# Graph-network kernel: four gather buffers instead of three, two PSUM banks for the sums, loops of four chunks

## The chip, the cores and the metric

One Trainium2 chip, one core of it. The metric is the device time of one execution in microseconds (us), the median of several. One profiled execution supplies the trace.

## What is computed

`N` = 6250 nodes with 256 features each, `E` = 100000 edges that are sorted by destination, four heads of 64. Two graph-attention layers run one after the other, beside them one linear attention over the nodes, and behind them a mixture of 16 experts (two per node). Cut to what matters here:

```
def gat_conv(x, src, dst, W, a_src, a_dst, b):
    h = (x @ W).reshape(-1, H, C)
    e = leaky_relu(alpha_s[src] + alpha_d[dst], 0.2)
    m = segment_max(e, dst)
    ex = exp(e - m[dst])
    s = segment_sum(ex, dst)
    out = segment_sum(h[src] * (ex / s[dst])[:, :, None], dst)
    return out + b

x = x + gat(relu(gat(xn))) + mix(xn)
x = x + experts(layernorm(x))
```

The `mix` part needs, over all nodes, the product of normalised keys and values (`dots`). Its keys and values are computed tile by tile inside the edge stage of the first layer.

## The kernel before

The program is a row of stages: prepare, project the inputs, find the maxima per destination, the edge stage of layer 0 (`gat_edges`, about 180 to 1400 us of the span), the maxima again, the edge stage of layer 1 (about 1435 to 2640 us), then the order of the experts, the experts and the finish (to the end).

An edge stage runs over `NC` = 98 chunks of 1024 edges and `NT` = 49 tiles of 128 nodes, one tile for every second chunk. Each engine writes its own instruction stream out by hand: `skewed` gives every engine a list of steps with an offset each, and turn t of an engine runs each step for chunk t minus its offset (for the tile steps only where that number is even, for the tile of half that number). The first and last turns are written out, the middle is a hardware loop with a body of 2 x `SLOTS` = 6 chunks, so that every buffer number is a constant in it.

What a chunk needs, in order:

- SP: `load` fetches the chunk's 1024 source numbers (`idx`, L880), after `logits` of the chunk three before. `load_codes` (L884) fetches the destination codes of the next chunk, spread to 128 partitions, after `hotT` of the chunk before. In layer 0 `load_x` (L894, offset 1) fetches the transposed node features of tile i after the keys and the values of tile i-3 have been computed, because there are `SLOTS` = 3 buffers `xnT`. In layer 1 `load_x` stands at offset 6 and waits for a much older step.
- POOL: `gather` issues 8 indirect DMAs of 128 rows by 260 fp32 (L926) into one of three buffers `G` ("gathered" in the trace). It waits for the chunk's `idx` and for `added` of the chunk three before, that is for the matmuls that read the buffer last.
- DVE: `edge_logits` (L974 reads the PSUM bank of `targets`, L977 adds the gathered part, L978, L979), `placed` (L983, the fp32 one-hot `hotf`, three buffers, waits for `added` of three before), `edge_scale` (L990, multiplies the gathered rows by the weights from ACT), `one_hot` of the chunk two ahead (L966 `hotT`, L607 and L608 `dwin`), `gain` of the chunk two before (L998, twice: PSUM sums into `acc`), and tile work (L1007, L1023, L1029 to L1032).
- PE: `targets` (L1204), keys (L1226), project, turn, dots (L1234), then `add` of the chunk before (L1212, the sum of 8 matmuls into one of three banks `psA`; it waits for `hotf`, for `scaled` and for `gain` of the chunk three before), values (L1220).

The wait for `gain` and the count that stands ready for it at the start are these:

```
dve.sem_inc(s["acc"], 2 * SLOTS)
pe.wait_ge(s["acc"], g * 2 + 2)
```

In layer 0 `targets` shares its bank with the weights, so PE waits there for `scaled` of the chunk before it.

Of the kernel before, what the change touches and what calls it, by code (L numbers as in the profile page):

```python
# [23 lines left out]
ds = bass.ds  # L24
# [10 lines left out]
CE = KT * P  # L35
SLOTS = 3
NC = -(-E // CE)
# [98 lines left out]
def build(nc, a, out):  # L136
# [15 lines left out]
    with ExitStack() as top:  # L152
# [27 lines left out]
        with ExitStack() as gnn:  # L180
# [6 lines left out]
            sq, ks = w1[:, 2], w1[:, 3, 0]  # L187
            vs = [w1[:, 11 + b, 0] for b in range(SLOTS)]
            xnT = [w1[:, 4 + b, 0, 0:C] for b in range(SLOTS)]
            wq, woutT, zmix = (w1[:, e].rearrange("p a (b f) -> p (a b) f", f=C) for e in (8, 9, 10))  # L190
# [565 lines left out]
def gat_edges(nc, layer, srcp, table, codes_d, partition, iota, acc, own, peak, parts, windows, attention, last, sem):  # L756
# [5 lines left out]
    with ExitStack() as ctx:  # L762
# [21 lines left out]
        rden = sb("rden", [P, H])  # L784
        psA = pb("psA_e", [P, SLOTS, 512])
        if attention:
            xnT_d, eps, wkvT, wq, woutT, zmix, sq, ks, vs, xnT, dotsT, mixM = attention
            a, table_out, ident, dtab, wext, scratch = last
            ss = sb("ss", [P, 3, 2 * MH])
            rkv = sb("rkv", [P, MH])  # L790
            psDW = pb("psDW_e", [P, 512])
            psD, psW = psDW[:, 0:6 * KT * H].rearrange("p (k c h) -> p k c h", c=3, h=H), psDW[:, 256:256 + KT * H]
            psKV = pb("psKV", [P, 2, MI])
            psM = pb("psM", [P, 512])
            psF = pb("psF", [P, 512])
            hidden, hidT = scratch[:, 0:C], scratch[:, C:2 * C].rearrange("p (k f) -> p k f", k=2)
            bias = scratch[:, 2 * C:2 * C + 2]
        else:
            a, xnT_d, xf_d, moe_d, ident, ones, eps, mixM, pair_hot, extra, w1, weights_in, scratch = last
            psD = pb("psD_e", [P, 2 * KT, 3, H])  # L800
            psW = pb("psW_e", [P, KT * H])
            psY = pb("psY", [P, 512])
            psX = pb("psX2", [P, 512])
            psG = pb("psG", [P, 512])
            taken = [0]

            def part(n):
                taken[0] += n
                return scratch[:, taken[0] - n:taken[0]]
            x = [part(C) for b in range(SLOTS)]  # L810
            xnT = [part(C) for b in range(SLOTS)]
# [12 lines left out]
        names = ["idx_in0", "idx_in1", "idx_in2", "g_in0", "g_in1", "g_in2", "codes_in0", "codes_in1", "hotT", "hotf", "targets", "dwin", "own", "own_weights",  # L824
                 "own_terms", "target_read", "logits", "weights", "scaled", "added", "acc", "pass", "dests", "dest_steps", "vsteps", "logit_steps", "tick",
                 "nears", "constants", "rden", "hidden", "fin_turned", "end"]
        if attention:
            names += ["xn_in0", "xn_in1", "xn_in2", "keys_ps", "values_ps", "squared", "kvsum", "kvroot", "ks", "vs", "dots", "key",
                      "relu", "projected", "out", "stored"]
        else:  # L830
            names += ["x_in0", "x_in1", "x_in2", "mixed", "halves", "moments", "yb", "root", "inverse", "scale", "xf", "stored", "xfT", "gated",
                      "gate_logits", "number", "gap", "exp", "bias"]
        s = {n: sem(f"g{layer}_{n}") for n in names}
        block = ctx.enter_context(nc.Block())
        assert NC == 2 * NT
        PER_STORE = 16 if attention else 32

        def chunks(eng, begin, end, *stages):
# [3 lines left out]
            with eng.Fori(0, rounds) as r:  # L842
                def told(step):
                    return lambda c, k, u: step(r * NC + c, c, k % SLOTS, k % 2, r * len(range(k % SLOTS, NC, SLOTS)) + u * 2 + k // SLOTS)

                def tile_of(step):

                    def even(c, k, u):
                        if k % 2 == 0:
                            b = k // 2  # L850
                            step(r * NT + (u * SLOTS + b), u * SLOTS + b, b, r * len(range(b, NT, SLOTS)) + u)
# [90 lines left out]
        def _(dve):  # L942
            dve.sem_inc(s["logits"], SLOTS)
            dve.sem_inc(s["target_read"], 1)
            dve.sem_inc(s["acc"], 2 * SLOTS)
            dve.sem_inc(s["hotT"], 2)
# [16 lines left out]
            def one_hot(g, c, q, par, use):  # L963
# [4 lines left out]
                chain.at(g * STEPS)  # L968
                blend(dve, chain, dwin[:, q, :], half[:, q, :], parts, tile, lower[:, ds(c, 1)], upper[:, ds(c, 1)]).then_inc(s["dwin"], 1)

# [21 lines left out]
            def gain(g, c, q, par, use):  # L992
                first = dve.value_load(window_tile[0:1, ds(c, 1)], min_val=0, max_val=NT)
                dve.wait_ge(s["added"], g + 1 + SLOTS)
                for half_of, mask in enumerate((lower, upper)):
                    dve.wait_ge(s["acc"], g * 2 + 2 * SLOTS)
                    into = acc[:, ds(first + half_of, 1), :].rearrange("p o f -> p (o f)")
                    dve.scalar_tensor_tensor(into, psA[:, q, 0:GW], mask[:, ds(c, 1)], into, ALU.mult, ALU.add).then_inc(s["acc"], 1)  # L998

            def denominators(t, i, b, use):  # L1000

                dve.wait_ge(s["hidden"], t + 1)
                if attention:
                    dve.wait_ge(s["out"], t * 2 + 2)
                hold(dve, s["acc"], t * 4 + (4 if isinstance(i, int) and i == NT - 1 else 6) + 2 * SLOTS, s["tick"])
                d = dest_of(dve, i)
                dve.reciprocal(rden[:], acc[:, ds(d, 1), C:GW].rearrange("p o h -> p (o h)")).then_inc(s["rden"], 1)  # L1007

            def next_pass(r):

                dve.wait_ge(s["acc"], r * (2 * NC) + 2 * NC + 2 * SLOTS)
                dve.tensor_scalar(code_r[:], code_r[:], -SPREAD, None, ALU.add).then_inc(s["pass"], 1)
# [7 lines left out]
            if attention:  # L1020
# [4 lines left out]
                def keys(t, i, b, use):  # L1025
# [4 lines left out]
                    key.link(dve.tensor_tensor(rkv[:], ss[:, 2, 0:MH], ss[:, 2, MH:2 * MH], ALU.mult))  # L1030
                    dve.wait_ge(s["dots"], t + SLOTS)
                    dve.tensor_tensor(ks.rearrange("p (g d) -> p g d", d=MD), psKV[:, 0, :].rearrange("p (g d) -> p g d", d=MD),  # L1032
# [5 lines left out]

                hold(dve, s["dots"], rounds * NT + SLOTS, s["tick"])
                for hp in range(4):  # L1040
# [7 lines left out]
            else:  # L1048
                steps = Chain(dve, s["end"])

                def stats(t, i, b, use):
                    hold(dve, s["mixed"], t + 1 + SLOTS, s["tick"])
                    dve.bn_stats(st, psY[:, 0:C]).then_inc(s["halves"], 1)
# [46 lines left out]
        def _(act):  # L1100
# [9 lines left out]
            def divide(t, i, b, use):  # L1110
                d = dest_of(act, i)
                act.wait_ge(s["rden"], t + 1)
                if not attention:
                    act.wait_ge(s["yb"], t + 1)
                act.wait_ge(s["fin_turned" if attention else "mixed"], t + (1 if attention else SLOTS))
                for h in range(H):
# [3 lines left out]
            if attention:  # L1120
                def squares(t, i, b, use):
                    act.wait_ge(s["keys_ps"], t + 1 + SLOTS)
                    act.wait_ge(s["values_ps"], t + 1 + SLOTS)
                    act.wait_ge(s["kvsum"], t + 1)
# [31 lines left out]
            else:  # L1156
                act.wait_ge(s["codes_in1"], 16)
                act.wait_ge(s["idx_in2"], 16)
                for e in range(0, NX - 4, 4):
# [33 lines left out]
        def _(pe):  # L1193
# [3 lines left out]
            def targets(g, c, q, par, use):  # L1197
# [5 lines left out]
                for k in range(KT):  # L1203
                    ins = pe.matmul(psD[:, 2 * k:2 * k + 2, :, :].rearrange("p g c h -> p (g c h)"), hotT[:, par, k, :], dwin[:, q, :], start=True, stop=True)  # L1204
                ins.then_inc(s["targets"], 1)

            def add(g, c, q, par, use):
# [3 lines left out]
                for k in range(KT):  # L1211
                    ins = pe.matmul(psA[:, q, 0:GW], hotf[:, q, k, :], G[:, q, k, :], start=(k == 0), stop=(k == KT - 1))  # L1212
                ins.then_inc(s["added"], 1)

            if attention:
# [29 lines left out]
                def project(t, i, b, use):  # L1245
# [19 lines left out]
            else:  # L1265
# [17 lines left out]
                def gates(t, i, b, use):  # L1283
# [4 lines left out]
                    ins.then_inc(s["gated"], 1)  # L1288
                pe.sem_inc(s["mixed"], SLOTS)
                pe.sem_inc(s["gated"], 1)  # L1290
# [469 lines left out]
```

## Time and profile before

| | |
|---|---|
| median of 3 runs | 3246.72 us (3243.73 to 3248.16) |
| profiled execution, its own time | 3252.82 us |
| its span in the profile | 3251.2 us |
| mean granted TensorE clock | 0.817 |
| PE busy | 2138.4 us, 66% |
| PE weight load busy | 1632.7 us, 50% |
| DVE busy | 1829.3 us, 56% |
| ACT busy | 931.8 us, 29% |
| POOL busy | 1934.7 us, 60% |

The shares are averages over stages that have different limits. Idle time before an instruction is put down to a releaser: another engine's instruction, a DMA, "remote" (a semaphore whose sender the profile doesn't name) or "issue" (nothing that the profile shows).

### The profile page before, as it was taken

The page shows a single profiled execution, that of the slowest core. Times are in us where ns is not written, and L with a number is a line of the kernel's source. Part 1 is how long each engine was busy: PE and PEld are TensorE (multiplying, and loading weights), DVE is VectorE, ACT ScalarE, POOL GpSimd, SP SyncE. Part 2 cuts the span into 40 slices and gives each one's busy share as a digit, 9 for nine tenths or more (in the row PEclk, how much of TensorE's full clock was granted, in tenths as well). Part 3 has the DMA queues.
Part 4 walks back from the last instruction along what each step waited for, and adds up shares of the span by engine and source line. Part 5 has one row for each costly group of instructions (what it writes and reads, how often), then busy time and mean ns, then how long its engine had stood idle before and what let it go on. Part 6 is the DMA issues. An engine that isn't in the chain of part 4 may idle for free. (4 is left out here: it accounts for less than half of the span.)

```text
span 3251.2 us, 50978 instructions
## 1 busy us (share of the span) xinstructions
PE 2138.4 (66%) x10263; PEld 1632.7 (50%) x10264; DVE 1829.3 (56%) x4382; ACT 931.8 (29%) x2254; POOL 1934.7 (60%) x1918
## 2 busy tenths in 40 slices
PE   1736676666666666635656666666576556999996
PEld 1424454444444444424444444444454436999984
DVE  5555565556556565555555555555555556555545
ACT  0502233223222232210122222222222224444445
POOL 0356666666666666626666666666666622676654
PEclk9968878778788888867777777777777778999998
DMA  3734444444444444425544444544445425555555
GB/s 82 212 94 118 119 120 119 123 123 118 118 121 116 118 120 121 114 78 170 134 132 133 134 128 128 139 128 136 131 128 139 131 72 141 104 104 105 103 93 168
DMA packets 273929, 399.38 MB, mean 123 GB/s; under 512 B 90592, under 2 KB 187255, under 8 KB 273849
## 3 DMA queue, kind: packets, MB, share of 16 engines
q0 software_dynamic: 101728, 251.76, 31.3%
q1 hardware_dynamic: 128457, 101.17, 11.4%
q10 hardware_dynamic: 43680, 45.76, 4.3%
q8 instruction: 21, 0.34, 0.0%
q14 instruction: 43, 0.35, 0.0%
HBM read 344.28 MB, written 54.62 MB: 123 GB/s over the span
## 5 line engine op out<-in xcount | busy, mean ns | idle before, releaser
L926 POOL DMA_INDIRECT gathered<-table,idx x1568 | 1583.7, 1010 | 808.9 <-issue 467.5
L1212 PE MATMUL psA_e<-gathered,hotf 128*128 128x260 f32 x3136 | 871.8, 437 | 93.8 <-issue 59.2
L1212 PEld LDWEIGHTS psA_e<-gathered,hotf 128*128 128x128 f32 x3136 | 692.3, 224 | 244.4 <-issue 115.6
L1107 ACT ACTIVATE gathered<-t_e 128x32 f32<-128x32 f32 x196 | 45.0, 230 | 1062.3 <-issue 649.4
L1623 POOL DMA_INDIRECT moe_d<-xscaled,xtarget x113 | 179.2, 1586 | 123.7 <-DVE xtarget L1567 54.8
L983 DVE TENSOR_TENSOR hotf<-iota,code_r 128x1024 f32<-128x1024 bf16 x196 | 240.2, 1226 | 5.1 <-issue 5.1
L998 DVE SCALAR_TENSOR_TENSOR acc<-psA_e,lower,acc 128x260 f32 x196 | 95.8, 489 | 259.4 <-issue 203.3
L1204 PE MATMUL psDW_e<-dwin,hotT 128*128 128x24 bf16 x784 | 38.4, 177 | 290.9 <-DVE gathered L990 236.1
L1595 PEld LDWEIGHTS xpsH<-xxT,w1e 128*128 128x128 f32 x1808 | 221.5, 193 | 6.2 <-ACT xxT L1524 0.4
L990 DVE TENSOR_TENSOR gathered<-gathered,psW_e 128x2048 f32<-128x2048 f32 x98 | 223.5, 2280 | 1.7 <-ACT gathered L1107 1.7
L990 DVE TENSOR_TENSOR gathered<-gathered,psDW_e 128x2048 f32<-128x2048 f32 x98 | 223.4, 2280 | 0.0
L1604 PE MATMUL xpsO<-w,hidT 128*128 x904 | 217.2, 383 | 7.8 <-DVE hidT L1556 7.2
L1595 PE MATMUL xpsH<-xxT,w1e 128*128 128x128 f32 x1808 | 222.1, 276 | 0.0
L1204 PEld LDWEIGHTS psDW_e<-dwin,hotT 128*128 128x128 bf16 x784 | 33.8, 101 | 345.7 <-issue 314.8
L1204 PE MATMUL psD_e<-dwin,hotT 128*128 128x24 bf16 x784 | 42.7, 175 | 220.6 <-issue 149.7
L1226 PE MATMUL psKV<-w 128*128 128x512 f32 x196 | 158.8, 956 | 41.6 <-DVE w L1032 40.1
L1556 DVE TENSOR_SCALAR hidT<-xpsH,b1T 128x128 f32<-128x128 f32 x452 | 127.4, 345 | 93.0 <-issue 43.0
L1604 PEld LDWEIGHTS xpsO<-w,hidT 128*128 128x128 f32 x904 | 163.8, 191 | 29.3 <-issue 11.0
L1220 PE MATMUL psKV<-w 128*128 128x512 f32 x196 | 115.4, 718 | 67.9 <-ACT w L1127 41.2
L977 DVE TENSOR_TENSOR z_e<-both_e,gathered 128x32 f32<-128x32 f32 x196 | 38.2, 195 | 209.0 <-DMA gathered<-table,idx 161.3
L1204 PEld LDWEIGHTS psD_e<-dwin,hotT 128*128 128x128 bf16 x784 | 35.2, 98 | 229.5 <-issue 193.3
L1614 POOL DMA_INDIRECT xx<-xf_d,xsource x113 | 111.4, 986 | 40.9 <-issue 33.0
(314 smaller groups left out, 3213.7 us busy)
## 6 DMA issues: line engine op xcount, KB each, us to landing
codes<-codes_d SPq DMA_DIRECT2D x196, 256.0 KB
gathered<-table,idx POOLq DMA_INDIRECT x1568
w<-in_L_ffn_w ACTq DMA_DIRECT2D x8, 2048.0 KB
xb<-in_L_ffn_b SPq DMA_DIRECT2D x113, 128.0 KB
w<-xnT_d SPq DMA_DIRECT2D x98, 128.0 KB
table<-acc POOLq DMA_DIRECT2D x49, 130.0 KB
table<-acc ACTq DMA_DIRECT2D x49, 130.0 KB
xnT_d<-xnT ACTq DMA_DIRECT2D x49, 128.0 KB
```

The costliest lines, as they stand in the source:

```text
L926: pool.indirect_dma_start(out=G[:, q, k, :], out_offset=None, in_=table, in_offset=bass.IndirectOffsetOnAxis(ap=idx[:, q, k:k + 1], axis=0 ...
L983: dve.tensor_tensor(hotf[:, q, :, :], iota[:].rearrange("p (k f) -> p k f", k=1).to_broadcast([P, KT, P]), code_r[:, ds(c * KT, KT)].rearr ...
L990: dve.tensor_tensor(f, f, w, ALU.mult).then_inc(s["scaled"], 1)
L1204: ins = pe.matmul(psD[:, 2 * k:2 * k + 2, :, :].rearrange("p g c h -> p (g c h)"), hotT[:, par, k, :], dwin[:, q, :], start=True, stop=True)
L1212: ins = pe.matmul(psA[:, q, 0:GW], hotf[:, q, k, :], G[:, q, k, :], start=(k == 0), stop=(k == KT - 1))
L1220: ins = pe.matmul(psKV[:, 1, :], xnT[b][:, kc * P:(kc + 1) * P], wkvT[:, kc, 1, :], start=(kc == 0), stop=(kc == 1))
L1226: ins = pe.matmul(psKV[:, 0, :], xnT[b][:, kc * P:(kc + 1) * P], wkvT[:, kc, 0, :], start=(kc == 0), stop=(kc == 1))
L1556: dve.tensor_scalar(hidT[:, q % 2, k * P:(k + 1) * P], psH[:, q % 2, k * P:(k + 1) * P], b1T[:, ds(e, 1), k:k + 1].rearrange("p o k -> p ( ...
L1595: ins = pe.matmul(psH[:, q % 2, k * P:(k + 1) * P], w1e[:, q % 2, kc, k * P:(k + 1) * P], xT[:, q % 2, kc, :], start=(kc == 0), stop=(kc = ...
L1604: ins = pe.matmul(psO[:, q % 2, 0:C], hidT[:, q % 2, k * P:(k + 1) * P], w2[:, ds(e, 1), k, :].rearrange("p o f -> p (o f)"), start=(k == ...
L1614: pool.indirect_dma_start(out=x[:, q, :], out_offset=None, in_=xf_d, in_offset=bass.IndirectOffsetOnAxis(ap=source[:, q:q + 1], axis=0)).t ...
L1623: pool.indirect_dma_start(out=moe_d, out_offset=bass.IndirectOffsetOnAxis(ap=target[:, q % 2:q % 2 + 1], axis=0), in_=scaled[:, q % 2, :], ...
```

## The change

Three things change together.

- `SLOTS` goes from 3 to 4. It now numbers the buffers of `G`, `hotf` and `idx` alone. `gather` waits for `added` of the chunk four before, `load` for `logits` of four before.
- What belongs to a tile (`xnT`, `x`, `vs`) goes from three buffers to `TURN` = 2, `dwin` and `half` from three to two, and `psA` from three banks to two. `load_x` of tile i waits for keys and values of tile i-2, and `add` waits for `gain` of the chunk two before.
- The loop body goes from 6 chunks to 4 (`SLOTS`). The offsets of the steps stay as they are.

```
-SLOTS = 3
+SLOTS = 4
+TURN = 2
...
-            vs = [w1[:, 11 + b, 0] for b in range(SLOTS)]
-            xnT = [w1[:, 4 + b, 0, 0:C] for b in range(SLOTS)]
+            vs = [w1[:, 11 + b, 0] for b in range(TURN)]
+            xnT = [w1[:, 4 + b, 0, 0:C] for b in range(TURN)]
...
-        dwin = sb("dwin", [P, SLOTS, 6 * H], BF16)
-        half = sb("half", [P, SLOTS, 6 * H], BF16)
+        dwin = sb("dwin", [P, 2, 6 * H], BF16)
+        half = sb("half", [P, 2, 6 * H], BF16)
...
-        psA = pb("psA_e", [P, SLOTS, 512])
+        psA = pb("psA_e", [P, 2, 512])
...
-                skewed(eng, NC, 2 * SLOTS, 2, 2, [(o, tile_of(step) if by_tile else told(step)) for o, step, *by_tile in stages])
+                skewed(eng, NC, SLOTS, 2, 2, [(o, tile_of(step) if by_tile else told(step)) for o, step, *by_tile in stages])
...
-            dve.sem_inc(s["acc"], 2 * SLOTS)
+            dve.sem_inc(s["acc"], 4)
...
-                    dve.wait_ge(s["acc"], g * 2 + 2 * SLOTS)
+                    dve.wait_ge(s["acc"], g * 2 + 4)
                     into = acc[:, ds(first + half_of, 1), :].rearrange("p o f -> p (o f)")
-                    dve.scalar_tensor_tensor(into, psA[:, q, 0:GW], mask[:, ds(c, 1)], into, ALU.mult, ALU.add).then_inc(s["acc"], 1)
+                    dve.scalar_tensor_tensor(into, psA[:, par, 0:GW], mask[:, ds(c, 1)], into, ALU.mult, ALU.add).then_inc(s["acc"], 1)
...
-                ins = pe.matmul(psA[:, q, 0:GW], hotf[:, q, k, :], G[:, q, k, :], start=(k == 0), stop=(k == KT - 1))
+                ins = pe.matmul(psA[:, par, 0:GW], hotf[:, q, k, :], G[:, q, k, :], start=(k == 0), stop=(k == KT - 1))
...
-                pe.sem_inc(s["dots"], SLOTS)
-                pe.sem_inc(s["values_ps"], SLOTS)
-                pe.sem_inc(s["keys_ps"], SLOTS)
+                pe.sem_inc(s["dots"], TURN)
+                pe.sem_inc(s["values_ps"], TURN)
+                pe.sem_inc(s["keys_ps"], TURN)
```

Two places in the order of instructions matter below. The first is SP's queue in the loop of layer 0. Semaphore names in brackets are those under which a number was first used; `g0_keys_ps,g0_values_ps` are the keys and values of this stage, the others stand for `logits` (before the fetch of `idx`) and for `hotT` (before the fetch of the codes). Before, at the end of the loop of six:

```order
96 L892 ISA
97 L894 ISA [waits g0_keys_ps,g0_values_ps]
98 L894 DMA w<-xnT_d 128x256
99 L880 REGISTER_ALU [waits i_first]
100 L880 DMA idx<-srcp 128x8
101 L59 ISA
102 L884 ISA [waits e_tiled]
103 L884 DMA codes<-codes_d 128x1024
104 L107 REGISTER_ALU
105 L107 COMPARE_AND_BRANCH
```

With the change, at the end of the loop of four:

```order
83 L893 ISA
84 L895 ISA [waits g0_keys_ps,g0_values_ps]
85 L895 DMA w<-xnT_d 128x256
86 L881 REGISTER_ALU [waits i_tick]
87 L881 DMA idx<-srcp 128x8
88 L60 ISA
89 L885 ISA [waits e_coded]
90 L885 DMA codes<-codes_d 128x1024
91 L108 REGISTER_ALU
92 L108 COMPARE_AND_BRANCH
```

The order has stayed: the fetch of the features of a tile, and behind it the fetch of the next even chunk's source numbers and of the codes. What moved is the tile whose keys and values the first one waits for, from i-3 to i-2.

The second is POOL's queue in the same stage. Before, three of the six gathers in the loop body (each with its wait for `idx` in the row ahead):

```order
71 L59 ISA [waits e_filled]
72 L926 DMA gathered<-table,idx 128x260 [waits g0_added]
73 L926 DMA gathered<-table,idx 128x260 x7
74 L59 ISA [waits e_loaded]
75 L926 DMA gathered<-table,idx 128x260 [waits g0_added]
```

With the change, the start of a body that holds four of them:

```order
65 L108 UNCONDITIONAL_BRANCH
66 L108 ISA
67 L60 ISA [waits e_stored]
68 L927 DMA gathered<-table,idx 128x260 [waits g0_added]
69 L927 DMA gathered<-table,idx 128x260 x7
```

Each chunk has the same 8 DMAs and the same two waits as before; the body has 12 rows where it had 18, and `g0_added` is waited for at a count that is lower by one chunk.

## Rows read from the trace of the kernel before

**Rows 1.** Windows: us, each engine's busy time (instructions), clock, DMA share, GB/s.

```profile
180.00:1400.00 1220.00, 799.55 (x3408) 544.27 (x3409) 707.10 (x1324) 339.23 (x817) 796.50 (x784) 0.81 0.43 117
...
1435.00:2640.00 1205.00, 729.52 (x3110) 557.43 (x3110) 662.80 (x1371) 257.56 (x667) 787.23 (x784) 0.75 0.49 135
```

**Rows 2.** Costliest groups on the page: busy, mean ns of one, idle before.

```profile
L926 POOL DMA_INDIRECT gathered<-table,idx x1568 | 1583.7, 1010 | 808.9 <-issue 467.5
```

**Rows 3.** Waits of POOL, 180 to 1400 us: total, times, longest.

```profile
POOL gathered L926 <- remote: 152.8, 48, 4.7
```

**Rows 4.** The same waits, 1435 to 2640 us.

```profile
POOL gathered L926 <- remote: 152.6, 44, 4.3
```

**Rows 5.** Timeline of POOL, 600 to 760 us (start, us, operation, count, idle before).

```profile
612.49 0.95 POOL L926 DMA_INDIRECT gathered<-table,idx  x1 [3.43 <-remote]
...
729.32 0.95 POOL L926 DMA_INDIRECT gathered<-table,idx  x1 [0.31 <-issue]
733.31 0.95 POOL L926 DMA_INDIRECT gathered<-table,idx  x1 [3.05 <-remote]
...
743.03 0.95 POOL L926 DMA_INDIRECT gathered<-table,idx  x1 [0.30 <-issue]
...
757.65 0.94 POOL L926 DMA_INDIRECT gathered<-table,idx  x1 [2.96 <-remote]
```

**Rows 6.** Timeline of PE, 712 to 742 us.

```profile
714.82 3.67 PE L1212 MATMUL psA_e<-gathered,hotf 128*128 128x260 f32 x16
725.51 0.37 PE L1204 MATMUL psDW_e<-dwin,hotT 128*128 128x24 bf16 x8 [7.02 <-DVE gathered L990]
...
731.96 3.67 PE L1212 MATMUL psA_e<-gathered,hotf 128*128 128x260 f32 x16
...
739.28 3.01 PE L1212 MATMUL psA_e<-gathered,hotf 128*128 128x260 f32 x13
```

**Rows 7.** Timeline of DVE, 717 to 747 us.

```profile
732.45 0.49 DVE L998 SCALAR_TENSOR_TENSOR acc<-psA_e,lower,acc 128x260 f32 x1 [4.83 <-issue]
732.86 0.48 DVE L998 SCALAR_TENSOR_TENSOR acc<-psA_e,upper,acc 128x260 f32 x1
733.25 0.35 DVE L974 TENSOR_REDUCE both_e<-psDW_e 128x64 f32<-128x192 f32 x1
...
739.95 0.48 DVE L998 SCALAR_TENSOR_TENSOR acc<-psA_e,upper,acc 128x260 f32 x1
...
745.80 0.19 DVE L977 TENSOR_TENSOR z_e<-both_e,gathered 128x32 f32<-128x32 f32 x1 [2.85 <-DMA gathered<-table,idx]
```

**Rows 8.** Timeline of SP's queue, 712 to 760 us.

```profile
715.81 0.70 SPq L894 DMA_DIRECT2D w<-xnT_d  x1
722.25 0.71 SPq L880 DMA_DIRECT2D idx<-srcp  x1
...
740.12 0.00 SPq L894 DMA_DIRECT2D w<-xnT_d  x1
```

**Rows 9.** Timeline of POOL, 826 to 880 us.

```profile
829.93 0.94 POOL L926 DMA_INDIRECT gathered<-table,idx  x1 [3.04 <-remote]
...
861.41 0.94 POOL L926 DMA_INDIRECT gathered<-table,idx  x1 [0.30 <-issue]
867.06 0.96 POOL L926 DMA_INDIRECT gathered<-table,idx  x1 [4.71 <-remote]
```

**Rows 10.** Timeline of DVE, 826 to 895 us.

```profile
865.93 0.36 DVE L974 TENSOR_REDUCE both_e<-psDW_e 128x64 f32<-128x192 f32 x1 [14.65 <-remote]
...
875.37 0.35 DVE L974 TENSOR_REDUCE both_e<-psDW_e 128x64 f32<-128x192 f32 x1
```

**Rows 11.** Timeline of SP's queue, start of the stage.

```profile
179.57 0.45 SPq L880 DMA_DIRECT2D idx<-srcp  x1
```

**Rows 12.** Timeline of POOL, the first gather.

```profile
183.54 2.77 POOL L926 DMA_INDIRECT gathered<-table,idx  x1 [5.68 <-issue]
```

**Rows 13.** Waits of SP's queue, 180 to 1400 us.

```profile
SPq L60 <- DVE t_e L979: 241.5, 48, 14.8
```

More of the change, by code:

```diff
@@ L809, in part @@
                 return scratch[:, taken[0] - n:taken[0]]
-            x = [part(C) for b in range(SLOTS)]
-            xnT = [part(C) for b in range(SLOTS)]
+            x = [part(C) for b in range(TURN)]
+            xnT = [part(C) for b in range(TURN)]
             hidden, xf, xfT, beta, gate = part(C), part(C), part(C), part(C), part(2 * NX).rearrange("p (k e) -> p k e", k=2)
@@ L823, in gat_edges @@
             one = sb("one", [P, NT])
-        names = ["idx_in0", "idx_in1", "idx_in2", "g_in0", "g_in1", "g_in2", "codes_in0", "codes_in1", "hotT", "hotf", "targets", "dwin", "own", "own_weights",
+        names = ["idx_in0", "idx_in1", "idx_in2", "idx_in3", "g_in0", "g_in1", "g_in2", "g_in3", "codes_in0", "codes_in1", "hotT", "hotf", "targets", "dwin", "own", "own_weights",
                  "own_terms", "target_read", "logits", "weights", "scaled", "added", "acc", "pass", "dests", "dest_steps", "vsteps", "logit_steps", "tick",
@@ L834, in gat_edges @@
         block = ctx.enter_context(nc.Block())
-        assert NC == 2 * NT
+        assert NC == 2 * NT and SLOTS == 2 * TURN
         PER_STORE = 16 if attention else 32
@@ L843, in told @@
                 def told(step):
-                    return lambda c, k, u: step(r * NC + c, c, k % SLOTS, k % 2, r * len(range(k % SLOTS, NC, SLOTS)) + u * 2 + k // SLOTS)
+                    return lambda c, k, u: step(r * NC + c, c, k, k % 2, r * len(range(k, NC, SLOTS)) + u)
                 def tile_of(step):
@@ L850, in even @@
                             b = k // 2
-                            step(r * NT + (u * SLOTS + b), u * SLOTS + b, b, r * len(range(b, NT, SLOTS)) + u)
+                            step(r * NT + (u * TURN + b), u * TURN + b, b, r * len(range(b, NT, TURN)) + u)
                     return even
                 begin(r)
-                skewed(eng, NC, 2 * SLOTS, 2, 2, [(o, tile_of(step) if by_tile else told(step)) for o, step, *by_tile in stages])
+                skewed(eng, NC, SLOTS, 2, 2, [(o, tile_of(step) if by_tile else told(step)) for o, step, *by_tile in stages])
                 end(r)
@@ L968, in one_hot @@
                 chain.at(g * STEPS)
-                blend(dve, chain, dwin[:, q, :], half[:, q, :], parts, tile, lower[:, ds(c, 1)], upper[:, ds(c, 1)]).then_inc(s["dwin"], 1)
+                blend(dve, chain, dwin[:, par, :], half[:, par, :], parts, tile, lower[:, ds(c, 1)], upper[:, ds(c, 1)]).then_inc(s["dwin"], 1)
             def edge_logits(g, c, q, par, use):
@@ L1004, in denominators @@
                     dve.wait_ge(s["out"], t * 2 + 2)
-                hold(dve, s["acc"], t * 4 + (4 if isinstance(i, int) and i == NT - 1 else 6) + 2 * SLOTS, s["tick"])
+                hold(dve, s["acc"], t * 4 + (8 if isinstance(i, int) and i == NT - 1 else 10), s["tick"])
                 d = dest_of(dve, i)
@@ L1009, in next_pass @@
             def next_pass(r):
-                dve.wait_ge(s["acc"], r * (2 * NC) + 2 * NC + 2 * SLOTS)
+                dve.wait_ge(s["acc"], r * (2 * NC) + 2 * NC + 4)
                 dve.tensor_scalar(code_r[:], code_r[:], -SPREAD, None, ALU.add).then_inc(s["pass"], 1)
@@ L1030, in keys @@
                     key.link(dve.tensor_tensor(rkv[:], ss[:, 2, 0:MH], ss[:, 2, MH:2 * MH], ALU.mult))
-                    dve.wait_ge(s["dots"], t + SLOTS)
+                    dve.wait_ge(s["dots"], t + TURN)
                     dve.tensor_tensor(ks.rearrange("p (g d) -> p g d", d=MD), psKV[:, 0, :].rearrange("p (g d) -> p g d", d=MD),
@@ L1037, in _ @@
                 rounds = chunks(dve, both_new(dve), next_pass, (1, edge_logits), (1, placed), (1, edge_scale), (6, keys, True), (-1, one_hot), (3, gain), (5, denominators, True), (5, sums, True))
-                hold(dve, s["dots"], rounds * NT + SLOTS, s["tick"])
+                hold(dve, s["dots"], rounds * NT + TURN, s["tick"])
                 for hp in range(4):
@@ L1051, in stats @@
                 def stats(t, i, b, use):
-                    hold(dve, s["mixed"], t + 1 + SLOTS, s["tick"])
+                    hold(dve, s["mixed"], t + 1 + TURN, s["tick"])
                     dve.bn_stats(st, psY[:, 0:C]).then_inc(s["halves"], 1)
@@ L1114, in divide @@
                     act.wait_ge(s["yb"], t + 1)
-                act.wait_ge(s["fin_turned" if attention else "mixed"], t + (1 if attention else SLOTS))
+                act.wait_ge(s["fin_turned" if attention else "mixed"], t + (1 if attention else TURN))
                 for h in range(H):
@@ L1121, in squares @@
                 def squares(t, i, b, use):
-                    act.wait_ge(s["keys_ps"], t + 1 + SLOTS)
-                    act.wait_ge(s["values_ps"], t + 1 + SLOTS)
+                    act.wait_ge(s["keys_ps"], t + 1 + TURN)
+                    act.wait_ge(s["values_ps"], t + 1 + TURN)
                     act.wait_ge(s["kvsum"], t + 1)
@@ L1157, in _ @@
                 act.wait_ge(s["codes_in1"], 16)
-                act.wait_ge(s["idx_in2"], 16)
+                act.wait_ge(s["idx_in3"], 16)
                 for e in range(0, NX - 4, 4):
@@ L1203, in targets @@
                 for k in range(KT):
-                    ins = pe.matmul(psD[:, 2 * k:2 * k + 2, :, :].rearrange("p g c h -> p (g c h)"), hotT[:, par, k, :], dwin[:, q, :], start=True, stop=True)
+                    ins = pe.matmul(psD[:, 2 * k:2 * k + 2, :, :].rearrange("p g c h -> p (g c h)"), hotT[:, par, k, :], dwin[:, par, :], start=True, stop=True)
                 ins.then_inc(s["targets"], 1)
@@ L1288, in gates @@
                     ins.then_inc(s["gated"], 1)
-                pe.sem_inc(s["mixed"], SLOTS)
+                pe.sem_inc(s["mixed"], TURN)
                 pe.sem_inc(s["gated"], 1)
```

4 lines of the change are left out of this document (2 added, 2 removed).

## The prediction

> **What bounds the kernel now.** I read the windows by stage first, then the waits of POOL in the two edge stages, then the timelines of POOL, PE, DVE and SP over two chunks. The edge stages take 1220 and 1205 us of the 3251.2 us span [rows 1]; the change touches nothing else. No engine is full in them. POOL is busy 796.5 and 787.2 us for 784 instructions [rows 1], 1010 ns each [rows 2], and the gap behind each gather is 0.30 us [rows 5]: a chunk of 8 gathers takes about 10.4 us and 98 of them 1020 us, more than PE's 800 or DVE's 707. POOL is the engine to look at, and what it loses beyond its own rate are the waits called "remote": 152.8 us in 48 places in layer 0, 152.6 us in 44 in layer 1 [rows 3, 4]. That is 3.2 to 3.5 us once in two chunks. The timeline shows the rhythm: seven resumes from 612.49 to 757.65 us, six periods, 24.2 us each [rows 5], that is 16 gathers (20.8 us) and one stop.
>
> **What ends a stop.** By the code the gather that resumes at 733.31 waits for the sum of the chunk three before. PE issued that sum at 714.82 and it took 3.67 us [rows 6], so it was done at 718.5, 15 us before the gather started. DVE's read at 733.25 [rows 7] waits for the small matmuls of 725.51 + 0.37 [rows 6], done 7 us before. Two waiters on two engines that were served long before, and both start just after POOL has stopped: its last gather ended at 729.32 + 0.95 = 730.27 [rows 5], DVE's `gain` starts at 732.45, the read at 733.25 [rows 7], the gather at 733.31. I read this so: while gathers run one behind the other, notices of completion from other engines arrive late, and they come in together some 2.2 us after the last gather. SP's queue has the same mark: a DMA issue takes 0.70 and 0.71 us at 715.81 and 722.25, none at 740.12 [rows 8]. By this reading a stop isn't a want of buffers, or only on its face: what POOL waits for was done, and it is the stop itself that lets the notice through.
>
> **The change, part by part**, against the profiled 3252.8 us (the median lies 6 us lower).
>
> *Four gather and one-hot buffers, layer 1.* If the reading holds, a fourth buffer lets POOL run on with a chunk more in hand once, but DVE and PE get their notices no sooner: they still work off about two chunks per stop, so POOL soon stands as often as before. Gain 0. Its bound on the other side is that all stops go: 152.6 us here, 152.8 us in layer 0, 305 us together.
>
> *Where the rule of the skill points.* The profile shows the same 3.2 to 3.5 us gap every two chunks on the engine nearest to saturation [rows 3, 4]. The Trainium skill, "Perfetto Trace Analysis", section Optimization Strategy, says that consistent bubbles on the engine that should be saturated can mean that SBUF or PSUM is short for the next tile; by that rule the change is right and the 305 us are within reach. It speaks against my forecast and is the first rival. The rows speak against it, because the buffer's last reader was done 15 us before the stop ended.
>
> *Two tile buffers, layer 0.* This is where I see a cost. SP's queue holds, in turn 2i+1, `load_x` of tile i, and right behind it the source numbers of chunk 2i+2. `load_x` now waits for the keys of tile i-2, which PE issues at its own turn 2i+1; before it waited for those of tile i-3, two turns earlier. So SP can't fetch the source numbers of an even chunk until PE has come to keys one turn before that chunk, and by the reading above SP hears of it only at the next stop. POOL's fourth buffer is of no use to the even chunks. Before, SP's main wait was for the logits of DVE (241.5 us in 48 places [rows 13]), ahead of the fetch itself and not ahead of `load_x`, which left the next numbers ready when the stop ended. Now a stop for an even chunk is, in a row: 2.2 us until the notice is there [rows 5, 7], 0.7 us for the issue of `load_x`, 0.7 us for that of `idx` [rows 8], about 2 us until the numbers are in SBUF, 0.3 us to start [rows 5]. The landing of `idx` is not in the trace by itself. Its lower bound is a gather's, from 743.03 + 0.95 = 743.98 [rows 5] to DVE's use at 745.80 [rows 7], 1.8 us; its upper bound is the first of the stage, from 179.57 + 0.45 = 180.02 to 183.54 [rows 11, 12], 3.5 us. I take 2.0, near the lower one, for the queue is short in the loop and cold at the start. The sum is 5.9 us against 152.8 / 48 = 3.2 before: +2.7 us a pair, times 47 pairs in the loop, 127 us. Stretches in which POOL stops for other reasons or runs three chunks on end [rows 9] won't pay it; I take three quarters, **+95 us**. Bounds: 0, if the numbers are there in time, and 47 x (2.7 + 1.5) = 197 us with the slow landing everywhere.
>
> *Two PSUM banks.* `add` of a chunk now waits for `gain` of two before, which DVE makes in the same turn in which it scales the chunk. PE issues the sum at 731.96, and the gain of that turn ends at 732.86 + 0.48 = 733.34: 1.4 us later. In the next turn 739.28 against 739.95 + 0.48 = 740.43: 1.15 us [rows 6, 7]. Behind `add` on PE stand the values and the next `targets`. DVE read the targets of 725.88 only at 733.25 and waits for a gather's landing at 745.80, so the shift is covered; if that cover were gone it would cost 1.3 us x 196 chunks = 250 us. DVE waits with `gain` for the sum, the sum for the gain of two before: no ring, but less play, where a notice is late. I put **+10 us** for both layers, near the covered end, with 0 and 250 us as ends.
>
> *`dwin`, `half` by parity:* both are written a turn ahead and read by the turn's `targets`, and DVE writes them again only behind its own read of that `targets` in the same turn, so no wait is added. 0. *Loops of four:* the same operations for each chunk, 12 rows of POOL in a body for 18; the branch comes every 4 chunks instead of 6, 7 more times in each stage on every engine, at the 0.30 us of a gap [rows 5] some 4 us for both, and beside other work. 0.
>
> The sum: +95 + 10 = +105 us, 3358 us for the profiled execution and **3352 us** for the median.
>
> **Rivals.**
>
> *A: the stops are a want of buffers and go (faster).* For it: the regular gap, the releaser is named by PE or not at all, and DVE at 9.4 us a chunk when all is there (865.93 to 875.37 [rows 10]) is quicker than POOL's 10.4. Against it: the done times above. If both layers lose all stops, 3247 - 305 = 2942 us. If layer 1 alone does and layer 0 pays the 95 us, 3247 - 153 + 95 = 3189 us; half of the stops in both and no cost of `load_x` is 3247 - 153 = 3094 us. I take about 3150 us as its middle. Chance 0.36, the largest single one after the forecast, because the chain from notices to the end of a stop is inferred, and because four buffers may let DVE find its data landed, where it now waits 2.85 us (745.80 [rows 7]).
>
> *B: no difference.* Four buffers shift the stops, `load_x` costs a little, both cancel within 0.2% of 3247, about 6.5 us, which is what a measurement of this kernel can tell from no change. Chance 0.10.
>
> *C: longer runs starve DVE (slower, another mechanism than mine).* With a fourth buffer POOL can run three chunks without a stop. It did so once in these rows: from 829.93 to a stop behind 861.41, resumed 867.06, which is 37.1 us for three chunks or 12.38 each [rows 9], while DVE stood 14.65 us [rows 10]. The rhythm of two has 24.2 / 2 = 12.10. If every run became one of three: 0.28 us x 196 = 55 us, 3302 us. It decides from the point where POOL has the third buffer at the resume. Chance 0.13.
>
> **How the numbers follow.** The forecast has 0.41, A 0.36, B 0.10, C 0.13. Slower by over 0.2%: 0.41 + 0.13 = 0.54. Faster: 0.36. Within: 0.10. Upward the range takes in the forecast with the slow landing everywhere, 3247 + 197 = 3444, rounded to 3440 us; above it, where `add` loses its cover, I leave 0.05. Downward it takes in C, B and the part of A in which at most half of the stops go, to 3094, rounded to 3090 us; some 0.15 of A's chance is below. The likeliest case alone lies between 3255 and 3440 us.
>
> **What would show it.** If I am right, layer 0's stage grows (1220 us to about 1315) and layer 1's hardly does (1205). POOL's remote waits in layer 0 stay near 48 and rise to about 5.9 us, or stand as waits for the DMA of `idx`; SP's queue shows long waits for keys (L1226) at `load_x`. Gathers still resume in runs of 16, with both DVE and POOL starting within a microsecond of each other. I am wrong if POOL's remote waits shrink in sum in either layer, if runs get longer than 16 gathers without DVE's read being held, or if SP's `idx` of an even chunk is issued while POOL is gathering. If layer 1 gains over 50 us, the reading of the late notices is the step that fails; if layer 1 stays and layer 0 stays too, it is the one on SP's queue.

## The result and the profile after

The changed kernel takes 3378.63 us (median of 4 runs, 3374.52 to 3386.28) beside 3247.44 us for the kernel before. The ratio is 1.0399, 95% interval 1.0378 to 1.0419: slower by 131 us. The profiled execution took 3374.52 us, span 3372.8, clock 0.808.

The windows view from the first to the last gather of each layer (us, each engine's busy time and instructions, granted clock, DMA share, GB/s). Before:

```profile
183.54:1379.40 1195.86, 786.45 (x3360) 535.83 (x3360) 693.20 (x1303) 330.64 (x795) 796.50 (x784) 0.81 0.44 119
1438.87:2623.14 1184.27, 714.83 (x3053) 546.46 (x3053) 649.97 (x1348) 251.57 (x649) 787.23 (x784) 0.75 0.50 136
```

After:

```profile
184.58:1474.20 1289.62, 855.03 (x3313) 564.70 (x3314) 689.87 (x1292) 324.18 (x786) 777.45 (x784) 0.78 0.41 110
1546.95:2735.31 1188.36, 689.39 (x3044) 516.00 (x3045) 649.31 (x1342) 251.04 (x647) 774.54 (x784) 0.77 0.49 135
```

Of the 121.6 us between the spans, layer 0's gathers have 1289.6 - 1195.9 = 93.7, layer 1's 4.1, the stretch between the layers 72.8 - 59.5 = 13.3, the stretch behind the last gather 637.5 - 628.1 = 9.4, and the start 1.0. The other 9.5 us of the 131 lie between the profiled executions and the medians: the one before is 5.4 us above its median, the one after 4.1 us below.

POOL's waits in layer 0 of the changed kernel (total, times, longest):

```profile
POOL gathered L927 <- DMA idx<-srcp: 260.5, 43, 6.6
...
POOL gathered L927 <- remote: 9.2, 2, 5.0
POOL gathered L927 <- PE psA_e L1213: 7.2, 2, 6.0
```

In place of the 152.8 us of "remote" waits [rows 3] (and 15.9 us on PE's sum, 168.7 in all) stand 260.5 us for the DMA of `idx`, 6.1 us each, 276.9 us in all (two of the expectations below have 269 for the 260.5). The waits grow by 108 us, the short gaps between gathers by 5 (236.3 to 241.0), and POOL's own busy time shrinks by 19 (796.50 to 777.45), which leaves the 94. SP's queue in the same stretch has what [rows 13] had not, 945.2 us at `load_x`:

```profile
SPq L894 <- remote: 945.2, 44, 24.3
SPq L61 <- DVE hotT L967: 94.3, 30, 21.8
SPq L894 <- PE psKV L1227: 30.8, 3, 11.0
```

Layer 1 has the remote waits of [rows 4] again, and more on PE's sum (12.6 us before) and on `idx` (7.4 before):

```profile
POOL gathered L927 <- remote: 147.4, 45, 5.9
POOL gathered L927 <- PE psA_e L1213: 37.6, 13, 4.2
POOL gathered L927 <- DMA idx<-srcp: 17.1, 5, 7.9
```

These waits grow from 172.6 to 202.1 us, while POOL's busy time and its short gaps shrink by 24 us; what is left is the 4.1.

One period of layer 0 in full. POOL's timeline of the changed kernel (start, us, operation, count, idle before):

```profile
735.00 0.94 POOL L927 DMA_INDIRECT gathered<-table,idx  x1 [6.23 <-DMA idx<-srcp]
...
754.43 0.95 POOL L927 DMA_INDIRECT gathered<-table,idx  x1 [0.30 <-issue]
761.54 0.95 POOL L927 DMA_INDIRECT gathered<-table,idx  x1 [6.16 <-DMA idx<-srcp]
```

The period is 761.54 - 735.00 = 26.5 us, for 24.2 before [rows 5]. PE in the same stretch:

```profile
745.62 0.35 PE L1205 MATMUL psDW_e<-dwin,hotT 128*128 128x24 bf16 x8 [2.45 <-DVE gathered L991]
746.72 3.57 PE L1227 MATMUL psKV<-w 128*128 128x512 f32 x4 [0.75 <-DVE w L1033]
...
752.22 0.38 PE L1213 MATMUL psA_e<-gathered,hotf 128*128 128x260 f32 x1 [0.81 <-issue]
753.65 0.38 PE L1213 MATMUL psA_e<-gathered,hotf 128*128 128x260 f32 x1 [1.05 <-issue]
755.06 0.47 PE L1213 MATMUL psA_e<-gathered,hotf 128*128 128x260 f32 x1 [1.03 <-issue]
757.87 5.79 PE L1213 MATMUL psA_e<-gathered,hotf 128*128 128x260 f32 x13 [2.34 <-issue]
```

DVE and SP's queue:

```profile
758.08 0.36 DVE L975 TENSOR_REDUCE both_e<-psDW_e 128x64 f32<-128x192 f32 x1 [8.56 <-DMA table<-acc]
```

```profile
758.32 0.33 SPq L895 DMA_DIRECT2D w<-xnT_d  x1
758.90 0.33 SPq L881 DMA_DIRECT2D idx<-srcp  x1
```

The last gather before the stop ended at 754.43 + 0.95 = 755.38. The keys of 746.72 end at 750.29. SP issues `load_x`, which waits for them, at 758.32: 8 us late, and 0.24 us behind DVE's read at 758.08. By the code that read waits for the targets of 745.62, done at 745.97; the profile names a DMA as its releaser, the last event that it saw. Then `idx` at 758.90 and the gather at 761.54. So the stop is 2.7 us until the notices are there, 0.24 + 0.58 us until SP has issued both, 2.64 us from the issue of `idx` to the gather: 6.16 us.

### The profile page after: what moved, and what is told of

Its sections match the earlier page's. It is cut to its first block and busy times, and to the rows that moved or that the text cites. A ratio compares the mean times of both kernels' runs of the same rounds, so it can differ in the third digit from the quotient of the medians.

```text
span 3372.8 us, 51370 instructions
## 1 busy us (share of the span) xinstructions
PE 2194.0 (65%) x10263; PEld 1639.6 (49%) x10264; DVE 1832.1 (54%) x4382; ACT 931.4 (28%) x2254; POOL 1902.3 (56%) x1918
## 3 DMA queue, kind: packets, MB, share of 16 engines
q0 software_dynamic: 101728, 251.76, 30.2%
## 5 line engine op out<-in xcount | busy, mean ns | idle before, releaser
L927 POOL DMA_INDIRECT gathered<-table,idx x1568 | 1552.0, 990 | 939.6 <-issue 460.6
L1213 PE MATMUL psA_e<-gathered,hotf 128*128 128x260 f32 x3136 | 939.1, 454 | 348.6 <-issue 206.5
L1213 PEld LDWEIGHTS psA_e<-gathered,hotf 128*128 128x128 f32 x3136 | 704.8, 230 | 558.2 <-issue 281.9
L975 DVE TENSOR_REDUCE both_e<-psDW_e 128x64 f32<-128x192 f32 x98 | 34.6, 353 | 375.2 <-DMA table<-acc 341.0
```

The lines of the kernel that those rows point to most:

```text
L927: pool.indirect_dma_start(out=G[:, q, k, :], out_offset=None, in_=table, in_offset=bass.IndirectOffsetOnAxis(ap=idx[:, q, k:k + 1], axis=0 ...
L1213: ins = pe.matmul(psA[:, par, 0:GW], hotf[:, q, k, :], G[:, q, k, :], start=(k == 0), stop=(k == KT - 1))
```

## The experiments

They ran on four chips, and chip by chip the kernel before took 2966, 3241, 2966 and 3227 us. Much of the argument rests on that difference. In each kernel below, unless its edit says otherwise, `dwin` and `half` have two buffers as in the change, and a loop of 12 chunks is there only so that two, three and four divide it. The sizes are set like this:

```
 SLOTS = 4     # G, hotf, idx
 TURN = 2      # xnT, x, vs
+BANKS = 2     # psA
+PERIOD = 4    # chunks in a loop body
```

**First chip (kernel before: 2966.04 us, 31 runs).** Three tile buffers again, the rest as changed (`TURN = 3`, `PERIOD = 12`):

> The change with three tile buffers again (xnT, x, vs); four gather buffers and two PSUM banks stay; loop of 12 chunks so that all numbers divide it. Load_x theory: layer 0 loses the 6 us stops for idx, its stops go back to about 3.2 us; the gathers of layer 0 take about 1200 us instead of 1290, total 3270 to 3290 us (the tails of a chunk more in hand stay). PSUM-bank theory, or that four gather buffers themselves cost it: stays at 3360 to 3385 us.

Measured 2956.33 us, ratio 0.9964 (0.9948 to 0.998). Two tile buffers alone (`SLOTS = 3`, `BANKS = 3`, `PERIOD = 12`):

> The kernel before with two tile buffers alone (three gather buffers, three PSUM banks, loop of 12). Load_x theory: layer 0 gets the wait for idx as in the change, 3320 to 3360 us. Rivals (banks, four buffers): 3247 us as before.

Measured 2973.76 us, ratio 1.0018 (1.0002 to 1.0034). Four gather buffers alone (`TURN = 3`, `BANKS = 3`, `PERIOD = 12`):

> Four gather and one-hot buffers alone: three tile buffers, three PSUM banks, loop of 12. Late-notice theory: a stop of about 3.2 us in two chunks stays in both layers, the sum of POOL's remote waits stays at about 300 us, 3250 to 3275 us. Want-of-buffers theory: the stops go, 3000 to 3150 us.

Measured 2958.69 us, ratio 0.9974 (0.9956 to 0.9993). Two PSUM banks alone (`SLOTS = 3`, `TURN = 3`, `PERIOD = 6`):

> The kernel before with two PSUM banks alone (three gather buffers, three tile buffers, loop of 6). Load_x theory: no effect beyond 10 us, 3245 to 3260 us. PSUM-bank theory: 3300 to 3380 us, with PE's sums waiting for gain.

Measured 2961.55 us, ratio 0.9987 (0.9973 to 1.0).

None of the expected times fits, for the ground is another: here every kernel is some 280 us faster, and POOL never stops. POOL's waits of the kernel with four gather buffers alone, whole execution:

```profile
POOL gathered L932 <- issue: 476.2, 1546, 5.6
```

Nearly all of the 476.2 us are gaps of 0.30 us between gathers. There is no "remote" wait at all, here or with three gather buffers (the second and fourth kernel). On this chip the edge stages run at the rate of the gathers, and no part of the change is worth more than 0.4%. The four runs can't tell the theories apart; they show that the 305 us of stops belong to some chips and not to the kernel alone.

**Second chip (kernel before: 3241.22 us, 18 runs).** The change as it is:

> The change as it is, once more, beside the kernel before. The experiments before this one ran on a chip on which the kernel before took 2966 us and POOL never stopped. Late-notice theory: the cost of the change depends on the stops, so where the kernel before takes about 2966 us the change costs under 10 us, and where it takes about 3247 us it costs 110 to 140 us. Theory that the longer wait of load_x costs by itself: over 60 us on either.

Measured 3367.72 us, ratio 1.037 (1.0336 to 1.0404): the result again, 126 us over the kernel before. POOL waits 236.6 us for `idx` in the whole execution (277.6 in the profile of the result). Three tile buffers again:

> The change with three tile buffers (four gather buffers, two PSUM banks, loop of 12). Where the kernel before takes about 3247 us: 3270 to 3290 us by the load_x theory, 3360 to 3385 us by the theory of the banks or of the fourth buffer itself. Where it takes about 2966 us: 2956 us again.

Measured 3253.01 us, ratio 1.0033 (1.0016 to 1.0049), under the forecast. POOL's waits, whole execution:

```profile
POOL gathered L932 <- remote: 285.5, 90, 5.9
...
POOL gathered L932 <- PE psA_e L1226: 41.9, 21, 3.9
...
POOL gathered L932 <- DMA idx<-srcp: 13.1, 6, 7.0
```

The waits for `idx` have gone from 236.6 us to 13.1, and the remote ones are back at 285.5. The third tile buffer gives back 115 of the 126 us. The fourth gather buffer and the two banks together cost 12 us; one of them could cost more if the other gains. Two tile buffers alone:

> The kernel before with two tile buffers alone (loop of 12). Where the kernel before takes about 3247 us: 3320 to 3360 us by the load_x theory, 3247 us by its rivals. Where it takes about 2966 us: 2974 us again.

Measured 3249.54 us, ratio 1.0025 (1.0006 to 1.0044). **The load_x theory, as I had put it, misses by 70 to 110 us.** `load_x` waits for the same keys as in the change, and it costs 8 us. POOL's waits, whole execution:

```profile
POOL gathered L932 <- remote: 249.0, 83, 4.3
POOL gathered L932 <- DMA idx<-srcp: 37.6, 10, 6.8
```

POOL, PE and SP's queue of this kernel:

```profile
701.05 0.95 POOL L932 DMA_INDIRECT gathered<-table,idx  x1 [2.94 <-remote]
...
724.91 0.95 POOL L932 DMA_INDIRECT gathered<-table,idx  x1 [3.07 <-remote]
```

```profile
707.21 3.62 PE L1240 MATMUL psKV<-w 128*128 128x512 f32 x4 [0.76 <-DVE w L1043]
```

```profile
711.05 0.33 SPq L899 DMA_DIRECT2D w<-xnT_d  x1
714.57 0.70 SPq L884 DMA_DIRECT2D idx<-srcp  x1
```

POOL resumes at 701.05. The keys come 6 us into the run and end at 710.83, and SP has their notice at 711.05, 0.2 us later, while POOL is gathering. In the change the keys come 11.7 us after the resume (746.72 against 735.00) and their notice is 8 us late.

One pair is not the layer. The table has all tiles between 250 and 1400 us (to 1530 for the last row, a kernel of the fourth chip), with the time from the end of the keys to SP's issue of `load_x`, from the timelines of PE and SP. SP can come to its wait later than the keys end, so a long time in the row of this kernel need not be a late notice.

| kernel | tiles | median | up to 1 us | 6 us or more |
|---|---|---|---|---|
| the change, result | 44 | 8.4 us | 2 | 41 |
| the change, second chip | 44 | 8.5 us | 2 | 42 |
| two tile buffers alone, second chip | 46 | 0.7 us | 24 | 7 |
| the change, third chip | 46 | 0.2 us | 44 | 0 |
| the change with four pauses, fourth chip | 47 | 0.2 us | 44 | 0 |

So notices are not late throughout a run, and in the change all 32 keys that ended over 13 us into one were. But the phase does not decide alone: of keys that ended 9 to 10.5 us into a run, all 6 were 13 us late in the change and 1 of 11 in this kernel. What else decides is open. That the change nearly always has the bad phase (45 of the 47 stops at the start of a chunk in layer 0 are before an even one, 30 of 52 before an odd one in the kernel before) fits its waits: the gather of an even chunk can only resume behind the keys, so the next keys are two chunks on, in the later part of the next run. This lock is argued, not shown by an edit of its own.

`load_x` one turn later in SP's queue:

```
-(0, load), (-1, load_codes), (1, load_x, True)
+(0, load), (-1, load_codes), (2, load_x, True)
```

> The change with load_x at offset 2 instead of 1, so that it stands in SP's queue behind the fetch of the source numbers of the even chunk. Where the kernel before takes about 3247 us, by the load_x theory: the odd chunk's numbers now stand behind it, which are needed 10 us later, so the 6 us stops shrink to about 3 us, 3270 to 3300 us. Rivals: stays at 3378 us. Where it takes about 2966 us: 2950 to 2966 us.

Measured 3273.38 us, ratio 1.0099 (1.0073 to 1.0125), within the forecast. POOL's waits, whole execution:

```profile
POOL gathered L932 <- remote: 269.4, 84, 5.1
...
POOL gathered L932 <- PE psA_e L1226: 62.2, 32, 4.0
...
POOL gathered L932 <- DMA idx<-srcp: 34.0, 16, 7.4
```

Waits for `idx` are 34.0 us, and the gathers of layer 0 take 1198.3 us (1195.9 in the kernel before, another chip). With two tile buffers, two banks and all else of the change kept, an order of SP's queue in which the keys' wait does not stand ahead of the even chunk's numbers gives back 94 of the 126 us. The edit also asks for the keys a turn later than the change does; order and turn are not separated. The loop has four chunks here as in the change and twelve in the two kernels before this one, so the loop is not what costs the 94 us.

**Third chip (kernel before: 2965.84 us, 25 runs).** The change as it is:

> The change as it is. Where the kernel before takes about 3245 us: 3360 to 3385 us, as measured. Where it takes about 2966 us: by the late-notice theory within 10 us of it, for no stop is there to be made longer; by the theory that load_x's longer wait costs by itself 60 us or more over it.

Measured 2968.43 us, ratio 1.0012 (0.9995 to 1.0028): within the 10 us. POOL's waits, whole execution, and one pair of PE and SP's queue:

```profile
POOL gathered L927 <- issue: 473.4, 1536, 5.6
...
POOL gathered L927 <- DMA idx<-srcp: 13.3, 18, 8.1
```

```profile
606.81 3.78 PE L1227 MATMUL psKV<-w 128*128 128x512 f32 x4 [0.73 <-DVE w L1033]
```

```profile
610.81 0.33 SPq L895 DMA_DIRECT2D w<-xnT_d  x1
611.39 0.33 SPq L881 DMA_DIRECT2D idx<-srcp  x1
```

The keys end at 606.81 + 3.78 = 610.59, SP issues `load_x` at 610.81. SP still stands 694.1 us in 47 places at that wait, but `idx` is issued at 611.39, in the middle of POOL's run, and is there long before its gather. Four gather buffers alone once more, meant for a chip with the stops and again on one without:

> Four gather and one-hot buffers alone (three tile buffers, three PSUM banks, loop of 12). Where the kernel before takes about 3245 us: late-notice theory 3240 to 3265 us, POOL's remote waits still about 300 us in sum; want-of-buffers theory 2950 to 3100 us. Where it takes about 2966 us: 2959 us again.

Measured 2957.53 us, ratio 0.9981 (0.9962 to 1.0001). So four gather buffers alone were never run where there are stops; the nearest is the kernel with three tile buffers on the second chip, which has two banks beside them. A pause of POOL ahead of each chunk in layer 0 of the change, on a tensor of its own that nothing reads (shortened):

```
 def gather(g, c, q, par, use):
+    if attention:
+        hold(pool, s["paused"], g + 1, s["tick"])
+        pool.tensor_scalar(pause, iota[0:1, 0:P].to_broadcast([1, 2, P]), 1.0, None, ALU.add).then_inc(s["paused"], 1)
```

> The change with a pause of POOL (one operation of about 3 us on a tensor of its own) ahead of each chunk's gathers in layer 0. Where the kernel before takes about 3245 us, by the late-notice theory: the notices get through in each pause, the keys' notice reaches SP in time, POOL's waits for idx (269 us in layer 0) fall under 60 us, and the pair takes 2 x (10.4 + 3.3) = 27.4 us for 26.5, in all 3400 to 3450 us. If load_x's wait costs whatever POOL does, the 6 us stops stay and the pauses come on top: 3600 to 3700 us. Where the kernel before takes about 2966 us: both give some 300 us over it.

Measured 2973.38 us, ratio 1.0023 (1.001 to 1.0036). The operation took 0.85 us and not 3, and the gathers, 1052 ns on average without it, took 970: where POOL works at the rate of the gathers, a small gap costs nearly nothing. It says nothing on late notices.

**Fourth chip (kernel before: 3227.06 us, 7 runs).** Four such operations ahead of each chunk (`for part in range(4)`, each on a slice of its own):

> The change with four small operations of POOL ahead of each chunk's gathers in layer 0 (0.85 us each in the run before this, so about 3.4 us for the four and 3.8 us with gaps). Where the kernel before takes about 3245 us, by the late-notice theory: the keys' notice reaches SP in a pause, POOL's waits for idx in layer 0 fall from 269 us to under 60 us, no chunk start waits 6 us, a pair takes 2 x (10.4 + 3.8) = 28.4 us for 26.5: 98 chunks at 14.2 us are 1392 us for 1290, about 3480 us in all. If load_x's wait costs whatever POOL does: the 6 us stops stay and 98 x 3.8 = 372 us come on top, about 3740 us. Where it takes about 2966 us: up to 372 us over it, less what the gathers gain by being spread (the single pause of 0.85 us cost 5 us in all).

Measured 3413.62 us, ratio 1.0583 (1.0562 to 1.0604). POOL's waits in layer 0:

```profile
POOL gathered L936 <- issue: 196.1, 643, 0.3
POOL gathered L936 <- POOL pause L932: 15.2, 92, 0.2
```

and in the whole execution, so in layer 1, which has no pauses:

```profile
POOL gathered L936 <- remote: 129.0, 41, 5.6
```

POOL, PE and SP's queue in layer 0:

```profile
714.59 3.30 POOL L932 TENSOR_SCALAR pause<-iota 1x256 int16<-1x256 bf16 x4
...
728.22 3.32 POOL L932 TENSOR_SCALAR pause<-iota 1x256 int16<-1x256 bf16 x4
```

```profile
721.95 3.78 PE L1236 MATMUL psKV<-w 128*128 128x512 f32 x4 [0.72 <-DVE w L1042]
```

```profile
725.95 0.68 SPq L897 DMA_DIRECT2D w<-xnT_d  x1
727.35 0.70 SPq L883 DMA_DIRECT2D idx<-srcp  x1
```

In layer 0 POOL waits for nothing but its own pauses: no `idx`, no sum. The keys end at 725.73 and SP issues `load_x` at 725.95, and so it is for 44 of 47 tiles (last row of the table). The chunk takes 13.6 us (714.59 to 728.22), which is 8 gathers and a pause of 3.5, and layer 0's gathers 1347.0 us. The forecast of 3480 us was too high by 66: 45 are the chunks, 1347.0 / 98 = 13.7 us each and not 14.2, and 20 the chip, on which the kernel before is that much faster. The rival's 3740 us are out. With the run of gathers broken every 10 us the notices are prompt, in an execution that has the stops where it is not broken; the price is higher than that of the stops (3.5 us a chunk for 3.2 us a pair), so it is a probe and no gain. The pauses also slow POOL down as a whole. Whether it is the break or the lower rate that helps is not separated.

No version that ran is faster than both kernels on both kinds of chip. Three tile buffers with four gather buffers is faster by 0.4% on the first chip and slower by 0.3% on the second.

## Why the prediction was right, and where it was not

- **What bounds it.** Right, with a limit that I could not see from one trace: POOL's gathers bound the edge stages, and what POOL waits for at a stop was done long before. For the stop at 733.31 that holds for both of its waits, as SP fetched the chunk's source numbers 23 us before:

```profile
710.18 0.34 SPq L880 DMA_DIRECT2D idx<-srcp  x1
```

  The kernels on the first and third chip have the same waits in their code and no stops, with three gather buffers as with four, and pauses take the stops away. That is why the first rival falls, with the limit that four gather buffers alone never ran where there are stops. "Late notices" is still a reading. In layer 0 of the change (the result) PE has gaps inside its sums too, between matmuls that wait for nothing by the code:

```profile
PE psA_e L1213 <- issue: 158.6, 125, 3.8
```

  The kernel before has 26.2 us of them in 24 places, and in the change on the third chip and with the four pauses this row does not appear. So the engines may get their own instructions late, and not only the notices of others; no run separates the two. Slower transfers of the gathers it is not: their DMA queue is busy for 30.2% of 3372.8 us in the result and for 34.6% of 2965.2 us in the change on the third chip, 1019 and 1026 us. The Trainium skill, "Perfetto Trace Analysis", section Optimization Strategy, says that a regular bubble can mean a want of SBUF or PSUM; here four gather buffers (with three tile buffers and two banks) have 285.5 us of it on a chip that has it, where the kernel before had 305.5 on another such chip, so the runs don't agree with that reading for this kernel.
- **Two tile buffers, +95 us in layer 0.** Measured +93.7. The stop was put at 5.9 us and is 6.1 on average where the profile names `idx`; in the period shown it is 2.7 us until the notices are there where I had 2.2, 0.82 us from there to the start of `idx`'s issue for 0.7, and 2.64 us from that to the gather for 0.7 + 2.0 + 0.3 = 3.0 (POOL stands, so SP's steps are 0.33 us). The factor of three quarters came out by luck: 45 of 49 pairs pay a stop before the even chunk, 5.95 us on average, so that the waits grow by 108 us, and what I took off for irregular stretches is in part POOL's busy time, 19 us less. The step that failed is "SP hears of it only at the next stop", stated for any kernel with `load_x` on keys of i-2. It held for 41 of 44 tiles in the change. On the second chip two tile buffers with three gather buffers and three banks cost 8 us, and SP had the keys' notice within 1 us for 24 of 46 tiles. With four gather buffers and two banks they cost 115. Which of these two it takes beside the two tile buffers is not separated.
- **The fourth gather buffer gives nothing in layer 1.** Right in the sum, +4.1 us, with all parts of the change in it: POOL waits 29.5 us more there, and its busy time and short gaps are 24 us less.
- **Two PSUM banks, +10 us.** Alone 0.9987 on a chip without late notices; with the fourth buffer 12 us on one with them. Not separated there. PE's sums do wait for `gain` in the profile after, 124.3 us in 62 places at L1213, of which 118.6 us are in layer 1. How much of that reaches POOL is not shown; its waits on the sums grow by 25 us there.
- **What I left out.** Between the 105 of the sum and the 131 lie the ends of the two layers, 13.3 + 9.4 us, and the 9.5 us between profiled executions and medians; layer 1 and the start (4.1 + 1.0) stand against the 10 us for the banks. With a fourth buffer POOL is a chunk further ahead of DVE when it is done, so more work stands behind the last gather. Of layer 0, before, POOL's last gather and DVE's last scaling:

```profile
1378.45 0.95 POOL L926 DMA_INDIRECT gathered<-table,idx  x1 [0.31 <-issue]
```

```profile
1383.39 2.28 DVE L990 TENSOR_TENSOR gathered<-gathered,psDW_e 128x2048 f32<-128x2048 f32 x1
```

After:

```profile
1473.26 0.94 POOL L927 DMA_INDIRECT gathered<-table,idx  x1 [0.30 <-issue]
```

```profile
1486.89 2.28 DVE L991 TENSOR_TENSOR gathered<-gathered,psDW_e 128x2048 f32<-128x2048 f32 x1
```

  1383.39 - 1379.40 = 4.0 us before and 1486.89 - 1474.20 = 12.7 us after. At the end of layer 1 it is 2.0 us more in the same way; the rest of the 22.7 us I have not traced. The second chip bears it out: this stretch is 4.4 and 4.7 us with three gather buffers and 6.4 to 16.9 us in the three kernels with four. Where there are no stops it is 4.2 and 4.3 us in the change.
- **Rival B** (no difference) is what happens on the chips without late notices, and **rival C** (longer runs) did not come about: 54 waits of over 0.6 us in layer 0 where there were 57.

## What to carry to other kernels

Where a queue holds a wait for one thing ahead of a fetch for another, taking one buffer from the first can delay the second, and four buffers of the second did not help here: look at what is queued behind a wait whose count the change moves. Before a stall is put down to a want of buffers, compare the end of the work waited for with the moment the waiter starts; if it was done long before, look for another cause before buying buffers. And a profile from one chip can hold a cost that another chip doesn't have, so repeat the kernel before beside each run.

## What was not expected of the hardware

- The same kernel took 2966 us on two chips and 3227 to 3247 us on the others, at a granted clock of 0.83 and 0.82, and the difference is near POOL's 305 us of stops. Why chips differ in this is open.
- On the latter, an engine can stand for microseconds while what it waits for is done and gathers run back to back: the keys that ended 15.3 us into a run were answered by SP 8 us later, those that ended 9.8 us into one 0.2 us later, and the late answers come 2.7 us after the last gather. The time into the run does not tell the two apart (9 to 10.5 us: 13 us late in the change, mostly prompt with two tile buffers alone). PE's own steps go slow then too: the sum that starts at 752.22 in the rows above has gaps of 0.81, 1.05, 1.03 and 2.34 us between matmuls and takes over 11 us, where it takes 3.67 us elsewhere [rows 6].
- On a chip without it, 0.85 us of other work of POOL per chunk shortened the gathers of layer 0 from 1052 to 970 ns on average, so that the change took 5 us more with it and not 98 x 0.85 = 83.
